# Causal self-attention taken by query halves on one NeuronCore: the order of the head groups, two heads to an exponential, row sums and maxima by halves

## The reference

```python
q = split(h @ Wq + bq)
k = split(h @ Wk + bk)
v = split(h @ Wv + bv)
att = jnp.einsum('bhqd,bhkd->bhqk', q, k) / jnp.sqrt(jnp.float32(hd))
causal = jnp.tril(jnp.ones((T, T), bool))
att = jnp.where(causal, att, -jnp.inf)
att = jax.nn.softmax(att, axis=-1)
y = jnp.einsum('bhqk,bhkd->bhqd', att, v)
y = y.transpose(0, 2, 1, 3).reshape(B, T, D)
return y @ Wp + bp
```

## Time and profile before

| | us |
|---|---|
| median of 3 runs (lowest, highest) | 3822.58 (3812.38, 3831.5) |
| the profiled execution, its own time | 3814.97 |
| its span in the profile | 3813.2 |
| last batch: first S tile to first ST tile | 989.5 to 1018.8 |
| last batch: groups 0, 1, 2, 3 of ST tiles | from 1018.8, 1052.0, 1089.8, 1126.0 to 1159.2 |

### The profile page before, as it was taken

One profiled execution on the slowest core, in us unless ns is written; L12 is line 12 of the kernel. 1 busy time (PEld: TensorE's weight loads), 2 busy tenths in 40 slices (PEclk: granted clock), 3 DMA queues, 4 the chain that ended last, 5 costly groups with the idle time before them and its releaser, 6 DMA issues. The chain is left out here.

```text
span 3813.2 us, 54364 instructions
## 1 busy us (share of the span) xinstructions
PE 3261.0 (86%) x20647; PEld 1791.2 (47%) x20647; DVE 2322.3 (61%) x5153; ACT 1558.8 (41%) x2500; POOL 466.6 (12%) x343
## 2 busy tenths in 40 slices
PE   7898798887886799988898888988888988879888
PEld 5434334334334689974463234553244632345532
DVE  8675776775764476665625667345756356673457
ACT  5355254354353355544524234433245242344332
POOL 0000001002003354440000210001300002100013
PEclk9799898898898899999998898998989998999999
DMA  7321511512516978862103120113021031201130
GB/s 274 81 47 43 152 28 48 139 28 57 142 22 104 269 245 252 260 168 57 29 14 54 36 57 18 23 29 74 12 57 29 15 53 35 57 17 23 29 74 12
DMA packets 207525, 301.54 MB, mean 79 GB/s; under 512 B 88924, under 2 KB 164198, under 8 KB 190120
## 3 DMA queue, kind: packets, MB, share of 16 engines
q1 hardware_dynamic: 186069, 273.20, 27.6%
q0 software_dynamic: 21184, 24.72, 3.5%
HBM read 215.13 MB, written 81.43 MB: 78 GB/s over the span
## 5 line engine op out<-in xcount | busy, mean ns | idle before, releaser
L963 PE MATMUL ps<-ternary_W,ident 128*128 128x512 f16 x1801 | 548.1, 412 | 48.2 <-SPq L604 13.5
L2314 DVE TENSOR_REDUCE max_parts<-ps 128x1 f32<-128x512 f32 (+3 forms) x608 | 374.7, 656 | 130.9 <-PE ps L1089 82.2
L2008 POOL TENSOR_TENSOR arena<-arena 128x640 f32<-128x640 f32 x108 | 175.7, 1627 | 1917.5 <-ACT arena L1915 1917.2
L1638 ACT ACTIVATE arena<-ps 128x1024 f32<-128x1024 f32 (+7 forms) x368 | 231.7, 651 | 273.3 <-PE ps L1109 203.9
L963 PEld LDWEIGHTS ps<-ternary_W,ident 128*128 128x128 f16 x1801 | 182.1, 104 | 310.0 <-issue 94.0
L2179 DVE CAST arena<-arena 128x256 f16<-128x256 f32 (+2 forms) x424 | 161.2, 380 | 251.5 <-ACT arena L1837 119.1
L1711 ACT ACTIVATE arena<-ps 77x1024 f32<-77x1024 f32 x192 | 190.6, 1017 | 201.1 <-PE ps L1284 198.4
L2778 DVE TENSOR_REDUCE max_parts<-ps 128x1 f32<-128x512 f32 x256 | 167.1, 686 | 137.9 <-PE ps L1495 137.0
L2181 DVE TENSOR_TENSOR arena<-arena 128x256 f16<-128x256 f32 (+2 forms) x424 | 236.4, 557 | 14.6
L1915 ACT ACTIVATE arena<-ps 128x1024 f32<-128x1024 f32 x128 | 130.7, 1024 | 249.3 <-PE ps L1511 249.3
L1837 ACT ACTIVATE arena<-ps,arena 128x256 f32<-128x256 f32 x312 | 147.2, 472 | 208.5 <-PE ps L915 208.5
(11 more groups left out here) (473 smaller groups left out, 7723.6 us busy)
## 6 DMA issues: line engine op xcount, KB each, us to landing
arena<-scr_expert_weights SPq DMA_DIRECT2D x52, 1024.0 KB, 7.6
k_stack<-scr_expert_weights SPq DMA_DIRECT2D x26, 1024.0 KB, 7.9
butterflied_W_exp<-in_exp_W SPq DMA_DIRECT2D x16, 1024.0 KB, 7.6
scr_expert_weights<-butterflied_W_con_turned SPq DMA_DIRECT2D x16, 1024.0 KB, 5.0
q_stack<-scr_q SPq DMA_DIRECT2D x108, 128.0 KB, 3.9
scr_q<-arena SPq DMA_DIRECT2D x48, 256.0 KB, 2.6
k_stack<-scr_q SPq DMA_DIRECT2D x72, 128.0 KB, 4.9
scr_q<-arena SPq DMA_DIRECT2D x16, 512.0 KB, 6.1
```

The costliest lines, as they stand in the source:

```text
L963: pe.matmul(s[:, 0:CH], ident[:], Wq1[:, 0, 0:CH], start=True, stop=True)
L1638: act.activation(PRs[n % NPC][:, kt * P:T], slot(L, "ST", g, kt, j)[:, kt * P:T], ACT.Exp).then_inc(*did("act", L, "exp", g, kt, j))
L2008: pool.tensor_tensor(total, p, total if kt > 1 else q, ALU.add).then_inc(*did("pool", "F3", "PA", h, kt))
L2314: dve.tensor_reduce(parts_by_head[:, j:j + heads, t, c], slot(L, "S", g, u)[:, 0:heads * n].rearrange("p (h n) -> p h n", n=n), AX, ALU.ma ...
```

## The change

The steps are now ordered by **places**: `ORDER` lists eight pairs (group, query half c), the first halves (queries 0 to 511, key tiles 0 to 3) of groups 0, 1, 2, then the second halves (queries 512 to 1023, key tiles 0 to 7) of groups 0, 1, 2, then both of group 3.

- An ST tile holds one key tile, one query half and **two** heads (side by side in a bank, or in two banks where a half is wider than 256), and one exponential takes both: 24 tiles and exponentials per group, where there were 32. The matmuls are the same.
- Only the 11 S tiles of the first place and 6 more stand ahead of the first ST tile; by the table `AHEAD` 16, 16, 16, 27, 27, 22 and 11 tiles are handed out beside places 0 to 6, none beside place 7.
- There are eight MT steps instead of four, each with four transposes of 4 x 128 (before one of 32 x 128), two copies on 4 partitions x 512 and two DMAs of longer runs; a first half's reductions write minus the maximum at once. All fillers in B0 are gone.
- Sums, RINV, NB and the multiplication come eight times on 512 queries instead of four times on 1024. SP now walks the list of steps too, so that the two DMAs of a row of sums no longer stand behind one another.
- Of the A steps of `AMONG`, moments, norm, first and second come beside S tiles in place 6, the others in place 7 up to key tile 4.
- Each expert piece is prepared one place earlier: piece 0 at the end of the batch before, 1 at the start of B0, 2 within place 7 (step X 2), 3 behind the last place (X 3). The last batch has none after its gate.

The rows that follow are instructions of one engine in the order of the program; names are those of the profile, widths those of the output.

The diff, cut:

```diff
+ORDER = [(0, 0), (1, 0), (2, 0), (0, 1), (1, 1), (2, 1), (3, 0), (3, 1)]
...
+AMONG = {(3, 0, 0, 0): ["moments"], (3, 0, 1, 0): ["norm"], (3, 0, 2, 0): ["first"], (3, 0, 3, 0): ["second"], (3, 1, 0, 0): ["third"],
+         (3, 1, 0, 1): ["softmax0"], (3, 1, 1, 0): ["softmax1"], (3, 1, 1, 1): ["softmax2"], (3, 1, 2, 0): ["softmax3"], (3, 1, 2, 1): ["softmax4"],
+         (3, 1, 3, 0): ["softmax5"], (3, 1, 3, 1): ["softmax6"], (3, 1, 4, 0): ["softmax7"]}
...
+SETS = [[(g, u) for u, unit in enumerate(UNITS) if unit[0] // (NT // 2) == c] for g, c in ORDER]
+AHEAD = [6, 22, 38, 54, 81, 108, 130, sum(len(x) for x in SETS[1:])]
+
+
+def score_block(c, kt):
+
+    a = max(kt * P, c * CH)
+    return a, (c + 1) * CH - a
...
+    ahead = [(g, u, i, n + 1 == len(x)) for i, x in enumerate(SETS) if i for n, (g, u) in enumerate(x)]
+    steps = [("S", g, u, "SB") for g, u in SETS[0]] + [("NM", 0)]
+    taken, due = [0], [(3, 0)]
+
+    def run_ahead(upto, ring):
+        while taken[0] < upto:
+            g, u, i, final = ahead[taken[0]]
+            steps.append(("S", g, u, ring))
+            taken[0] += 1
+            if final:
+                steps.append(("NM", i))
+                due.append((taken[0] + 2, i))
+            while due and due[0][0] <= taken[0]:
+                steps.append(("MT", due.pop(0)[1]))
+
...
+    for i, (g, c) in enumerate(ORDER):
+        while due and due[0][1] <= i:
+            steps.append(("MT", due.pop(0)[1]))
+        blocks = [(kt, score_block(c, kt)[1]) for kt in range(NT // 2 * (c + 1))]
+        whole, passed = sum(w for _, w in blocks), 0
+        for kt, w in blocks:
+            mine = [("ST", g, c, kt, 0), ("ST", g, c, kt, 1)] + ([("PV",) + before] if before else [])
+            before = (g, c, kt)
+            ring = "SX" if w <= CH // 2 else "S"
+            for n, step in enumerate(mine):
+                steps.append(step)
+                if i < LAST:
+                    share = (passed + w * (n + 1) / len(mine)) / whole
+                    run_ahead(int(AHEAD[i] + (AHEAD[i + 1] - AHEAD[i]) * share + 0.001), ring)
...
+                        steps.extend(difference_steps(part, ring))
+            passed += w
+            if i and kt == 1:
+                steps.append(("RINV", i - 1))
+            if i and kt == 3:
+                steps.append(("NB", i - 1))
+            if i == LAST and kt == 3:
+                steps.append(("X", 2))
...
+    steps.append(("PV",) + before)
...
+                store_expert(1)
+                sp.dma_start(stack_q[2][48:MROW], A["c_qs"][:, 0]).then_inc(*did("ld_const2", 0))
...
+                sp.wait_ge(*of("st_wexp0", 1))
+                sp.dma_start(stack_k[2][48:MROW + 2], A["c_ks"][:, 0]).then_inc(*did("ld_const2", 1))
...
-                max_rows(L, 0)
-                store_expert(1)
-                sp.dma_start(stack_q[2][48:MROW], A["c_qs"][:, 0]).then_inc(*did("ld_const2", 0))
-                sp.wait_ge(*of("st_wexp0", 1))
-                sp.dma_start(stack_k[2][48:MROW + 2], A["c_ks"][:, 0]).then_inc(*did("ld_const2", 1))
...
+                for s in own_attention_steps(led.batch > 0, more):
+                    if s[0] == "MT":
+                        max_rows(L, s[1])
+                    elif s[0] == "PV" and s[3] == NT // 2 * (s[2] + 1) - 1:
+                        sums_out(L, ORDER.index(s[1:3]))
+                        if s[1:3] == (0, 1):
+                            stacks(L, True, 3)
+                        if s[1:3] == (1, 1) and more:
...
+                            sp.wait_ge(*of("pe", L, "ST", 2, 1, NT - 1, 1))
...
+                        if more:
+                            load_expert(led.batch + 1, 0)
...
+                if b == 0:
+                    store_expert(0)
+                    load_expert(0, 1)
                 own_attention("B0")
...
+                    led.batch = b + 1
+                    store_expert(0)
+                    load_expert(b + 1, 1)
...
-                        pe.transpose(s[0:GH * NT, 0:P], negm[:, g % 2, :], identf[:]).then_inc(*did("pe", L, "MT", g))
+                        i = g
+                        s = claim("S", L, "MT", i)
+                        pe.wait_ge(*(of("dve", L, "negm", i) if ORDER[i][1] else of("dve", "free", L, "S", *SETS[i][-1])))
+                        for t in range(NT // 2):
+                            mm = pe.transpose(s[0:GH, t * P:(t + 1) * P], negm[:, i % 2, GH * t:GH * (t + 1)], identf[:])
+                        mm.then_inc(*did("pe", L, "MT", i))
...
+                        c, kt, j = step[2:]
+                        a, w = score_block(c, kt)
+                        s = claim("AU" if w <= CH // 2 else "A", L, "ST", g, c, kt, j)
...
-                            busy(s, 2 if g else 6)
-                            pe.wait_ge(*of(f"ld_m{mbuf}", L, g, 1))
...
+                            i = ORDER.index((g, c))
+                            pe.wait_ge(*of(f"ld_m{i % 2}", L, i, 1))
+                        for n in range(2):
+                            o = s[:, n * w:(n + 1) * w] if w <= CH // 2 else s[:, n * CH:n * CH + w]
+                            edge = a == kt * P
...
-                        mm.then_inc(*did("pe", L, "ST", g, kt, j))
+                                mm = pe.matmul(o[:, 0:P], big[:], causal[:, 1, :], start=False, stop=True)
...
+                            mm = pe.matmul(acc[QUARTER * j:QUARTER * (j + 1), a - c * CH:CH], VP[:, g, kt, j, :], p, start=kt == 0, stop=final,
...
+                        i = g
+                        s = claim("AQ", L, "NB", i)
+                        pe.wait_ge(*of(f"ld_r{ORDER[i][0]}", L, ORDER[i][1]))
+                        pe.matmul(s[:, 0:CH], E4[:], OT[i], start=True, stop=True).then_inc(*did("pe", L, "NB", i))
...
+                        scores = slot(L, "ST", g, c, kt, j)[:, 0:2 * w if w <= CH // 2 else 2 * CH].rearrange("p (h n) -> p h n", h=2)[:, :, 0:w]
+                        act.activation(PRs[n % NPC][:, 0:2 * w].rearrange("p (h n) -> p h n", h=2), scores, ACT.Exp).then_inc(*did("act", L, "exp", g, c, kt, j))
+                        released((L, "ST", g, c, kt, j), "act", (L, "exp", g, c, kt, j))
...
-                    elif step == ("RINV", NG - 1):
-                        expert_hi(2)
+                    elif step[0] == "X":
+                        expert_hi(step[1])
...
+                        i = ORDER.index(step[1:3])
+                        act.wait_ge(*of("pe", L, *step))
+                        if i >= 4:
+                            act.wait_ge(*of("dve", L, "onf", i - 4))
+                        act.activation(OT[i], slot(L, "PVacc", *step[1:3]), ACT.Copy).then_inc(*did("act", L, "ot", i))
...
-                expert_hi(0)
+                expert_hi(1)
                 q_k_f32(L)
...
-                expert_hi(3)
+                if b + 1 < NB:
+                    led.batch = b + 1
+                    expert_hi(0)
+                    led.batch = b
...
+                if half:
+                    if (g, u) == SETS[i][0] and g:
+                        dve.wait_ge(*of("dve", L, "negm", ORDER.index((g - 1, 1))))
+                    dve.tensor_reduce(parts_by_half[:, row, j:j + heads, c], scores, AX, ALU.max).then_inc(*frees("dve", L, "S", g, u))
+                else:
+                    dve.tensor_reduce(negm[:, i % 2, 0:GH * NT // 2].rearrange("p (t j) -> p t j", j=GH)[:, row, j:j + heads], scores, AX, ALU.max,
+                                      negate=True).then_inc(*frees("dve", L, "S", g, u))
...
+            def half_rows(L, i):
+                dve.wait_ge(*of("pe", L, "MT", i))
+                if i:
+                    dve.wait_ge(*of(f"ld_m{(i - 1) % 2}", L, i - 1, 1))
+                dve.tensor_copy(mhalf[:, 0], slot(L, "MT", i)[0:GH, 0:CH]).then_inc(*step(L, "mhi", i))
+                dve.wait_ge(*of("dve", L, "mhi", i))
+                dve.tensor_tensor(mhalf[:, 1], slot(L, "MT", i)[0:GH, 0:CH], mhalf[:, 0], ALU.subtract).then_inc(*step(L, "mrow", i))
+                released((L, "MT", i), "dve", (L, "mrow", i))
...
+                expert_lo(1)
...
+                    elif s[0] == "NM":
+                        if ORDER[s[1]][1]:
+                            minus_max_rows(L, s[1], last, GH * NT // 2)
                     elif s[0] == "MT":
-                        minus_max_rows(L, s[1], last, GH * NT)
-                        minus_max_parts(L, s[1], GH * NT)
-                        if s[1] == 0:
-                            expert_lo(1)
+                        half_rows(L, s[1])
+                    elif s[0] == "X":
+                        expert_lo(s[1])
                     elif s[0] == "A":
```

226 lines of the change are left out of this document (85 added, 141 removed).

## The result

The changed kernel takes 3834.14 us (median of 16 runs, 3822.8 to 3843.67) where the kernel before takes 3822.97 (16 runs beside it): a ratio of 1.0036, interval 1.0024 to 1.0047. That is slower by 14 us by the ratio and by 11 us by the medians; by the half per cent of the prediction it is no change, but 23 us less were forecast.

The account below looks back on a forecast made before the run. PE, busy 86%, was taken to bound the whole, with phase 0's stretches having own limits. Terms of -5.4 us per batch, times four -21.6, with -5.5, +6 and -2.3 gave -23.4: 3815 to 3792 us, range 3745 to 3850.

Parts of the forecast that it names:

- the term for the A steps: Phase 0: A steps lie closer together beside fewer ST tiles; 2 us added in three batches, +6 us.
- Ahead of the first exponential: Start of each batch: transposes wait for 11 S tiles instead of 38, 27 x 0.567 = -15.3 us per batch.
- the two constant loads: On SP ahead of the first row DMAs: hidden while S tiles run; without that cover some 2.5 us each.
- Stacks: S tiles' 10.6 us wait for stacks: 2.6 us given back in three batches, as the 1 MB load goes.
- Waits on exponentials: ST matmuls waiting for earlier exponentials, 8 us per batch: halved, -4 us per batch (0 to -8).
- Rival C: Phase 0: PE and ACT still wait in turn, terms -4 and -2.9 go, no change, 3820 us; chance 0.15.
- Handover of place 7: Last S tile to place 7's ST: DVE work and row DMAs 6.8 us, less 1.3 of PE's work, +5.5 per batch.
- rival B: Clock falls at handovers of places 3, 4, 5, 7 without fillers: 16 x 1.7 = 27 us, 3819 us; chance 0.12.
- Places 0 to 2: First halves of groups 0 to 2: DVE 11 us against PE's 10, a microsecond open in each, +3 per batch.
- rival A: Beside places 1 to 5 DVE becomes the limit, moved tiles cost 0.567 us each, 3843 us; chance 0.16.
- the phases behind: Sign: phases 1 and 2 keep their length.
- the last batch's first S tile to first ST tile: Sign at the last batch's start: this stretch falls from 29.3 us to about 14.

Follow-up runs that it names:

- experiment 2: Changed kernel with first transposes directly behind place 0's 11 tiles: ratio 1.0047; then also the first rows of maxima ahead of the third stack's loads: 1.0020.
- experiment 4: Changed kernel with 20 fillers in PE's wait ahead of place 7, nothing else: ratio 1.0036 to the kernel before.
- experiment 3: Changed kernel with 6 more S tiles beside places 4 and 5, the last 5 in place 6's first half, last transposes directly behind: ratio 0.9968.

## Why the prediction was wrong

The step that failed is the term for the A steps, +6, with 22 of the 38 us by which the places were mis-sized; the second is the clock, which the sum left out at place 0 and place 7.

- **Ahead of the first exponential**: -15.3 per batch was forecast, -14.1 came (56.4 / 4). That it came so near is luck in part. The 4.0 us (in the last batch) that the first transposes wait behind the tiles of the second stack were in no term. With the transposes ahead of that wait and the rows ahead of the third stack's loads, which I did not count either, it is 12.5 to 13.3 us (experiment 2), about -18 per batch. No run shows a cost of the two constant loads.
- **Stacks**: I gave back 2.6 us in three batches because the 1 MB load went. Instead the wait of S tiles rose from 10.6 to 16.0 us: with 11 tiles ahead in place of 38 PE reaches the second stack after 5 us, before it has landed:

```profile
1013.44 0.29 PE L1122 MATMUL ps<-k_stack,q_stack 96*128 96x128 f16 x1 [4.02 <-DMA k_stack<-scr_k]
```

- **Waits on exponentials**: -4 per batch forecast, 31.9 - 14.8 = 17.1, or -4.3, came. Rival C is out.
- **Handover of place 7**: +5.5, PE idles 5.1. The step was right but incomplete: the clock behind it costs 2 us more (experiment 4), and removing handover and clock was worth 26 us with what that did in place 6 (experiment 3).
- **Clock**: this was rival B, with the right mechanism at the wrong places. I priced the waits of places 3, 4 and 5 too; these last 0.6 to 1.0 us and the clock stays at 1.00 there. Place 0 I had not listed at all: its ten fillers were taken as gone at no cost ("which mostly fill a wait"). There the clock fell with the 4.0 us wait for the second stack (0.85 from 1009 to 1013 us, 0.50 from 1013 to 1021); it was 0.50 still in the two windows from 1021 to 1029 and 0.59 in the next, and 2.6 to 3 us per batch came back with it. In the kernel before, with the fillers, it was back at 1.00 soon behind the first ST tile (1018.8):

```profile
1017.00:1021.00 4.00, 4.00 (x17) 1.73 (x15) 0.95 (x3) 1.02 (x1) 0.00 (x0) 0.64 0.89 240
1021.00:1025.00 4.00, 3.45 (x20) 1.47 (x20) 3.88 (x8) 3.08 (x4) 0.00 (x0) 1.00 0.92 192
```

What B takes from the Trainium skill ("TensorE: Matmul & The Clock Gate", section "HAM oscillation — how this bites in real kernels") tells of pieces of matmul work shorter than the wait behind each. Here the places last 13 to 37 us and the waits 0.6 to 5.4, so that "By that rule the four handovers would pay each time" did not follow from it, and of the four only place 7 paid.
- **Places 0 to 2**: I took 12 us each; at full clock they take 13.0, 13.9 and 14.8 (16.0 and 16.1 in the two batches in which the clock of place 2 was 0.89). That is the size of rival A in part, but not shown to be its cause: DVE is busy for 83, 88 and 92% of them at full clock and PE for 90, 89 and 84%. From place 3 on DVE is at 83% or less and rival A fails.
- **The A steps**: this is the step that failed. "The A steps lie closer together beside fewer ST tiles; ... I add 2 in three batches", +6. The attention stretch of the first three batches, less three times that of the last, was 476.6 - 417.6 = 59.0 us and is 551.1 - 464.4 = 86.7: +27.7. In the kernel before, DVE takes the moments behind the last reduction, as the last group begins, and the inverse root beside that group, and PE's transposes come late enough to find both done. In place 6 both stand among reductions of S tiles, and PE waits for them. Of the 27.7 us some 15 are the wait of transposes for the scaling, as the scaling one step ahead shows; I had counted the A steps' instructions but not what stands behind them on PE.

The sum against the profile: 38 us more in the places than forecast (90.0 where the terms give 4 x 11.5 + 6 = 52), of which the A steps are 22 and the last batch's kind of loss 4 x 4.1 = 16, and some 5 us at the front. Of the signs named ahead, PE's wait at place 7 (5.1 us, 4 to 7 named), the halved waits on exponentials and the phases behind (2.4 us longer) came about as said; the last batch's first S tile to first ST tile took 16.65 us, not about 14. The clock at place 0 (2.6 to 3 us per batch) and at place 7 (2) is as large as that loss of the last batch. What stays open is the rest of the A steps' cost, about 12 us in three batches: wherever they were put it came back in part, and no run separates ACT's share from PE's.

## What to carry to other kernels

When a step is moved, list who waits for each of its results, and how much work stands between the step and its first reader on the reader's engine: here a serial chain cost nothing where it was done before the reader came up, and up to 6.6 us where it began late or the reader followed soon, even beside work that needs nothing from its engine. Filler matmuls are not waste to be summed up: what they are worth is read in the granted clock of the stretch behind the wait that they fill. When a small DMA is put on a path, look for the large ones issued just ahead of it on the same queue.

## What was not expected of the hardware

- Two row DMAs of the same size took 2.5 us from issue to use with no load of 128 KB or more issued in the 8 us ahead of them, 6.4 us when six loads of 128 KB each had been issued 3 to 6 us ahead, and 3.1 us when the same loads were 7 to 10 us old.
- The copies of 4 x 512 took 0.68 us, those of 128 x 512 from PSUM (L2393, a product) 0.69: 124 idle partitions saved nothing.
- At the start of place 0 the clock stood at 0.50 for 8 us, in which PE worked 7.4:

```profile
1021.00:1025.00 4.00, 3.74 (x14) 1.64 (x15) 1.92 (x3) 1.02 (x1) 0.00 (x0) 0.50 0.00 0
1025.00:1029.00 4.00, 3.66 (x23) 2.35 (x22) 1.98 (x3) 1.49 (x2) 0.00 (x0) 0.50 0.00 0
```
